# An accumulating transfer in place of a product for the global attention row of a transformer block

## The reference

```python
h = layernorm(x) * (1 + ca) + sa            # ca, sa, ga: one row of 512 per sequence
xs = h.reshape(4, 16, 128, 512)             # segments of 128 tokens
local = softmax(Q K^T * SCALE) V            # inside each segment
summ = xs[:, :, 0, :]                       # the first token of each segment
global_out = softmax(Qg Kg^T * SCALE) Vg    # among the 16 first tokens of a sequence
out = local + global_out[:, :, None, :]     # one row is added to all 128 tokens of a segment
x = x + ga * (out @ Wo.T + bo)              # ga: gate row, at least 0.25 in size
```

## Time and profile before

| | |
|---|---|
| median of 3 runs | 1911.46 us (1911.04 to 1913.74) |
| the profiled execution, its own time | 1909.39 us |
| span of that execution, first to last instruction | 1907.7 us |
| TensorE busy | 1821.5 us, 95% |
| DVE busy | 1226.4 us, 64% |
| POOL busy | 869.4 us, 46% |
| ACT busy | 822.3 us, 43% |
| mean granted TensorE clock | 0.985 of full speed |
| HBM read and written | 237.71 MB, 50.72 MB |

### The profile page before, as it was taken

The page is one execution under the profiler, slowest core; times in us unless marked ns, Lnnn a source line. Parts: engine busy times, 40 slices in busy tenths (PEclk is TensorE's granted clock), DMA queues, the critical chain, the costliest instruction groups (busy, mean ns, idle before and its releaser), DMA issues.

```text
span 1907.7 us, 28124 instructions
## 1 busy us (share of the span) xinstructions
PE 1821.5 (95%) x9137; PEld 1490.8 (78%) x9138; DVE 1226.4 (64%) x1877; ACT 822.3 (43%) x1321; POOL 869.4 (46%) x709
## 2 busy tenths in 40 slices
PE   8999999999999729999999999999998999999998
PEld 3477777778778527889888888888887988888886
DVE  4277888888888745455664544547748887454762
ACT  2445455455455314324443333435545654334541
POOL 2035665666666441244442334335636757233632
PEclk9999999999999969999999999999999999999999
DMA  8034234224224423444534354344545555434622
GB/s 271 29 135 156 89 113 153 89 95 170 88 90 149 162 92 108 144 144 166 178 125 154 127 173 139 122 148 163 185 161 180 191 186 187 170 124 154 214 86 66
DMA packets 137915, 270.77 MB, mean 142 GB/s; under 512 B 17633, under 2 KB 18221, under 8 KB 137862
## 3 DMA queue, kind: packets, MB, share of 16 engines
q1 hardware_dynamic: 115338, 221.27, 33.4%
q0 software_dynamic: 22528, 48.86, 8.0%
HBM read 237.71 MB, written 50.72 MB: 151 GB/s over the span
## 4 chain that ended last, share of the span: by engine, by line
PE 80%; DVE 11%; issue 4%; ACT 2%; POOL 1%; DMA 1%; DVEq 0%; POOLq 0%; ACTq 0%; SPq 0%
PE bank L322 23%; PE bank L324 23%; PE bank L323 23%; PE bank L771 2%; PE bank L707 2%; DVE h L1374 1%; DVE prob L1268 1%; DVE stats L1150 1%; DVE xr L1378 1%; PE bank L814 1%; PE bank L564 1%; PE bank L603 1%; DVE ht_lo L1214 1%; PE bank L532 1%; DVE u_lo L1396 1%
## 5 line engine op out<-in xcount | busy, mean ns | idle before, releaser
L1435 DVE TENSOR_TENSOR h_lo<-h_f,h_hi 128x512 fp32r<-128x512 f32 x256 | 223.5, 894 | 362.7 <-ACT h_f L1087 362.4
L1086 ACT ACTIVATE h_hi<-bank,b_col 128x512 fp32r<-128x512 f32 x256 | 176.7, 690 | 597.6 <-PE bank L324 581.8
L322 PE MATMUL bank<-bt_hi,w_hi 128*128 128x512 f32 (+4 forms) x1024 | 360.5, 352 | 8.4 <-DVE w_lo L1406 6.6
L324 PE MATMUL bank<-bt_hi,w_lo 128*128 128x512 f32 (+4 forms) x1024 | 359.5, 351 | 0.0
L323 PE MATMUL bank<-bt_lo,w_hi 128*128 128x512 f32 (+4 forms) x1024 | 359.3, 351 | 0.0
L322 PE MATMUL bank<-w_hi,h_hi 128*128 128x512 f32 x832 | 326.5, 392 | 2.8 <-DVE h_lo L1435 2.4
L323 PE MATMUL bank<-w_lo,h_hi 128*128 128x512 f32 x832 | 324.9, 390 | 0.0
L324 PE MATMUL bank<-w_hi,h_lo 128*128 128x512 f32 x832 | 324.7, 390 | 0.0
L322 PEld LDWEIGHTS bank<-bt_hi,w_hi 128*128 128x128 f32 x1024 | 194.7, 190 | 34.0 <-issue 9.0
L323 PEld LDWEIGHTS bank<-bt_lo,w_hi 128*128 128x128 f32 x1024 | 194.7, 190 | 20.9
L324 PEld LDWEIGHTS bank<-bt_hi,w_lo 128*128 128x128 f32 x1024 | 194.6, 190 | 20.3
(11 more groups left out here) (252 smaller groups left out, 3264.1 us busy)
## 6 DMA issues: line engine op xcount, KB each, us to landing
raw<-in_L_ffn_W_dram SPq DMA_DIRECT2D x128, 1024.0 KB, 6.9
xa<-in_L_attn_x_dram SPq DMA_DIRECT2D x16, 1024.0 KB, 5.4
xr<-in_L_attn_x_dram SPq DMA_DIRECT2D x16, 1024.0 KB, 7.9
out_dram<-xr SPq DMA_DIRECT2D x16, 1024.0 KB, 9.8
h_rows<-h SPq DMA_DIRECT2D x16, 1024.0 KB, 4.3
b_bc<-in_L_ffn_b_dram SPq DMA_DIRECT2D x16, 256.0 KB, 6.3
wm_b<-in_L_wmod_dram SPq DMA_DIRECT2D x2, 1024.0 KB, 8.2
wm_d<-in_L_wmod_dram SPq DMA_DIRECT2D x2, 1024.0 KB, 5.2
```

The source lines that it names most:

```text
L322: pe.matmul(o, a_hi, b_hi, start=start, stop=False)
L324: return pe.matmul(o, a_lo, b_hi, start=False, stop=stop)
L1086: act.activation(h1_hi[b % 2][:, j, :], h_bank[j][:, :], ACT.Relu, bias=bias)
L1435: dve.tensor_tensor(h1_lo[b % 2][:, j, :], h1_f[:, j, :], h1_hi[b % 2][:, j, :].bitcast(F32), ALU.subtract) \
```

## The change

The gated global row is added to the residual instead of the bank. The prologue loads the floored gate row of each sequence back from HBM to the 16 partitions of its segments (`g_ga`), DVE multiplies the global rows by it in float32, and SP stores the 64 rows (`global_rows`, now float32, one row each). In the attention phase POOL, at the head of its iteration, waits for the load of `xr` of group i-1 and issues one transfer that reads the group's four rows for every partition and adds them to `xr` (1 MB, `accum_op=ALU.add`). DVE waits for that transfer (`xr_summed`) ahead of the first gate product in place of the load. Gone are line 735's product, `seg_sel`, `grows`, its loads and the three parts.

```diff
-    global_dram = nc.dram_tensor("global_rows", (NSEG * 3, D), BF16, kind="Internal").ap()
+    global_dram = nc.dram_tensor("global_rows", (NSEG, D), F32, kind="Internal").ap()
...
-    seg_sel = keep("seg_sel", [P, GS, P], BF16)
-    grows = [keep(f"grows{i}", [P, D], BF16) for i in range(2)]
...
@@ sync
-        sp.wait_ge(g_split_done, 1)
-        sp.dma_start(global_dram.rearrange("(n t) d -> n t d", t=3), g_split[:]).then_inc(g_stored, 16)
-
         sp.wait_ge(mod_fixed, 2)
         sp.dma_start(mod_dram[:, 0:VC, :], modr[:, 0:VC, :]).then_inc(mod_stored, 16)
         sp.wait_ge(mod_stored, 16)
+        for b in range(NBATCH):
+            seg = slice(b * (NSEG // NBATCH), (b + 1) * (NSEG // NBATCH))
+            sp.dma_start(g_ga[seg, :], mod_dram[b:b + 1, GA, :].to_broadcast([NSEG // NBATCH, D])).then_inc(g_ga_in, 16)
 
         sp.wait_ge(pro_evac, PRO_END)
         sp.dma_start(ga_tab[:], spread(GA, P)).then_inc(late_tab_in, 16)
+        sp.wait_ge(g_gated, 1)
+        sp.dma_start(global_dram, g_ga[:]).then_inc(g_stored, 16)
         sp.wait_ge(g_stored, 16)
         sp.dma_start(cb_tab[:], spread(CB, P)).then_inc(late_tab_in, 16)
...
             if cur:
-                wait_past(sp, av_full, 4 * i.n - 4)
-                sp.dma_start(grows[i.par][0:3 * GS, :], global_dram[bass.ds(i.n * 3 * GS, 3 * GS), :]) \
-                    .then_inc(grows_in[i.par], 16)
@@ tensor
-                pe.wait_ge(grows_in[p1.par], 16 * (p1.half + 1))
...
-                    split3(pe, big[s][:, :], pt_hi[:, s, :], pt_lo[:, s, :], u_hi[:, s, :], u_lo[:, s, :], True, False)
-                    pe.matmul(big[s][:, :], seg_sel[:, s, :], grows[p1.par][:], start=False, stop=True) \
+                    split3(pe, big[s][:, :], pt_hi[:, s, :], pt_lo[:, s, :], u_hi[:, s, :], u_lo[:, s, :], True, True) \
                         .then_inc(av_full, 1)
@@ vector
-        dve.memset(grows[0][:], 0.0).then_inc(init_made, 1)
-        dve.memset(grows[1][:], 0.0).then_inc(init_made, 1)
...
-        dve.wait_ge(pro_evac, TG + 1)
-        dve.tensor_copy(g_split[:, 0, :], g_a[:]).then_inc(gsum_step, 1)
-        dve.wait_ge(gsum_step, 8)
-        dve.tensor_tensor(g_x[:], g_a[:], g_split[:, 0, :], ALU.subtract).then_inc(gsum_step, 1)
-        dve.wait_ge(gsum_step, 9)
-        dve.tensor_copy(g_split[:, 1, :], g_x[:]).then_inc(gsum_step, 1)
-        dve.wait_ge(gsum_step, 10)
-        dve.tensor_tensor(g_split[:, 2, :], g_x[:], g_split[:, 1, :], ALU.subtract).then_inc(g_split_done, 1)
         floor_gate(GB)
         dve.sem_inc(mod_fixed, 1)
         dve.wait_ge(pro_evac, PRO_END)
+        dve.wait_ge(g_ga_in, 16 * NBATCH)
+        dve.tensor_tensor(g_ga[:], g_a[:], g_ga[:], ALU.mult).then_inc(g_gated, 1)
         dve.wait_ge(tab_in, 16)
...
-                dve.wait_ge(xr_in[p1.par], 16 * (p1.half + 1))
+                dve.wait_ge(xr_summed[p1.par], 16 * (p1.half + 1))
@@ gpsimd
-        pool.memset(seg_sel[:], 1.0).then_inc(made, 1)
...
         def iteration(i, prev, nxt, prev3):
             p1 = i.plus(-1)
             b = batch_of(p1)
+            if prev:
+
+                if isinstance(i.n, int) and i.n == 1:
+                    pool.wait_ge(g_stored, 16)
+                pool.wait_ge(xr_in[p1.par], 16 * (p1.half + 1))
+                stand_alone(pool, pool_passed)
+                part = global_dram[bass.ds(p1.n * GS, GS), :].unsqueeze(0).to_broadcast([P, GS, D])
+                pool.dma_start(xr[p1.par][:], part, accum_op=ALU.add).then_inc(xr_summed[p1.par], 16)
             if nxt:
                 normalise1(i.plus(1))
```

More of the change, by code:

```diff
@@ L198, in build_block @@
                                       ("bqk", [NBATCH, 2, D], F32), ("hg_t", [P, KC, NSEG], F32))
-    g_split, brow, u_row, gg_t = over(r_tab + 8 * KB, ("g_split", [NSEG, 3, D], BF16), ("brow", [1, D], F32),
+    g_ga, brow, u_row, gg_t = over(r_tab + 8 * KB, ("g_ga", [NSEG, D], F32), ("brow", [1, D], F32),
                                       ("u_row", [1, D], F32), ("gg_t", [P, KC, NSEG], F32))
@@ L261, in build_block @@
     gsum_masked, gsum_negb, gsum_exp, gsum_prob = (sem(f"gsum_{k}") for k in ("masked", "negb", "exp", "prob"))
-    g_split_done, g_stored, table_cleared = sem("g_split_done"), sem("g_stored"), sem("table_cleared")
+    g_ga_in, g_gated, g_stored, table_cleared = (sem(k) for k in ("g_ga_in", "g_gated", "g_stored", "table_cleared"))
     x_in = [sem(f"x_in{i}") for i in range(2)]
     xr_in = [sem(f"xr_in{i}") for i in range(2)]
-    grows_in = [sem(f"grows_in{i}") for i in range(2)]
+    xr_summed = [sem(f"xr_summed{i}") for i in range(2)]
     ln1_step, ln1_ready, ln1_rstd, xn_done = (sem(k) for k in ("ln1_step", "ln1_ready", "ln1_rstd", "xn_done"))
@@ L335, in build_block @@
     LAST_POOL_SEG = GS - 1
-    POOL_MADE = 9
-    DVE_MADE = 8
+    POOL_MADE = 6
+    DVE_MADE = 6
     def results_done(eng, e, b):
@@ L1273, in query_const @@
                 .then_inc(qc_ready, 1)
-        dve.wait_ge(g_split_done, 1)
         tok4 = [P, GS, E]
@@ L1532, in _ @@
         pool.memset(ones[:], 1.0).then_inc(made, 1)
-        pool.memset(seg_sel[:], 1.0).then_inc(made, 1)
-        pool.wait_ge(made, 3)
+        pool.wait_ge(made, 2)
         pool.affine_select(out=tri[:], in_=tri[:], compare_op=ALU.is_gt, fill=0.0, base=0, pattern=[[1, P]],
                            channel_multiplier=-1).then_inc(made, 1)
[L1539 to L1543, removed]
         pool.iota(tokids[:], pattern=[[P, NSEG]], base=0, channel_multiplier=1).then_inc(made, 1)
```

## The result

The changed kernel took 1920.44 us (median of 6 runs, 1918.90 to 1922.78), the kernel before 1912.91 beside it (6 runs, 1911.04 to 1913.74): a ratio of 1.0041, interval 1.0028 to 1.0054. It is slower by 7.5 us. The prediction had 1928 with a range of 1912 to 1975, slower with a chance of 0.83. The direction was right and the measured time lies in the range; the forecast change, 16.3 us, was twice the measured 7.5. The profiled execution took 1919.15 us, its span 1917.5 against 1907.7, its mean granted clock 0.981 against 0.985.

What follows compares the result with a forecast made beforehand. DVE's chain up to u_lo was taken to pace the groups, though TensorE is busiest. Terms -1, +6.6, +1.7, +1, +6 and +2 sum to +16.3 us on 1911.46: 1928 us, range 1912 to 1975.

Steps and rivals of the forecast that it cites:

- The prologue, +6.6 and +1.7: Before the first group: DVE's wait for gate rows and product delay statistics 6.6 us; TensorE's half clock afterwards adds 1.7.
- hidden: Prologue: first xr load goes near 114, the sum lands by 133, before DVE wants it at 133.9.
- The transfer's price, 10.8 us from POOL's end to landing: Steady groups: issuing 1.3, h2 store 2.7, moving 5.4, landing 1.4; sum there 0.6 us ahead of DVE.
- Forecast (A): Whole kernel: transfer hidden but for the last group, 1928 us, own range 1916 to 1938; chance 0.47.
- (B): Attention phase: the sum comes late in every group, 1957 us, at the high ends 1983; chance 0.36.
- The slots of L735, -1: Attention loop: DVE's five waits for L735 give back one slot each, 1.2 us at most, taken as 1.
- rival (C): Attention loop: TensorE is the bound, u_lo is there before it reaches L603; all 64 slots return, 1905 us; chance 0.07.
- The sign that was asked for: Attention loop: distance of L1374 from group to group unchanged near 36 us, 499 in 14 groups.
- The second group, +1: Second group of the attention phase: margin of 9.9 us where the transfer needs 10.8, so 1 us late.
- Collisions of POOL and DVE, +2: Four early groups: POOL's L1608 comes sooner and lengthens the fourth query constant, 0 to 4.4 us, taken as 2.
- The last group, +6: End of attention phase: weight loads take half the DMA engines, moving doubles to 10.8 us, sum 6 us late.
- Its sign of being wrong: Last group: the prediction is wrong if the weight loads leave the transfer its full rate.

Runs made afterwards that it cites:

- Experiment 7: Prologue of experiment 6 and last transfer of experiment 8, with cb and sb tables loaded behind the store of the gated global row: 1908.29 us, 0.9985 to the kernel before.
- experiment 5: Changed kernel with DVE's product of global row and gate moved behind group 0's statistics, u_lo and query constants: 1919.5 us, ratio 1.0041 to the kernel before.
- experiment 3: Changed kernel with the transfer copying the rows over xr instead of adding them; only the attention phase compared: 14 distances 499.47 us against 500.00.
- experiment 4: Changed kernel with POOL issuing the transfer behind the four normalisations of its iteration instead of ahead of them: 2037.97 us in one run.
- experiment 1: Changed kernel with a fourth product per segment, of ones with zeros, put back on TensorE: 1923.72 us, ratio 1.0064 to the kernel before.
- experiment 2: Changed kernel without the accumulating transfer, DVE waiting for the xr load; only the attention phase compared: 1910.42 us, ratio 0.9992 to the kernel before.
- experiment 9: Changed kernel with the first expert weights' loads held back until the last group's transfer has landed: 1920.48 us in one run.
- experiment 6: Changed kernel with experiment 5's later product, its operand in own memory, first xr load behind the tables, product's store behind group 2's x load: 1916.11 us, ratio 1.0020.
- experiment 8: Changed kernel with the last group's accumulating transfer alone issued one iteration earlier: 1918.45 us, ratio 1.0028 to the kernel before.

## Why the prediction was right, and where it was too large

- **The prologue, +6.6 and +1.7: right in the mechanism, a little small.** The statistics were late by 7.73, of which 1.25 was there ahead of the change's first transfer, so 6.5. The half clock cost 1.5, but 2.6 in three kernels with the same prologue, more than the upper bound of 2. Together 8.9 to 9.2 for 8.3. Experiment 7 takes all of it away by order alone. What the prediction missed is that the same delay lay twice, in DVE's order and in SP's queue: it wrote of the first xr load "hidden" with 0.9 us to spare, and experiment 5 shows it as the next wait, once the first is gone.
- **The transfer's price, 10.8 us from POOL's end to landing: right within 0.7.** Measured 10.1. Its parts: issuing 1.0 for 1.3, moving 5.1 for 5.4. The Trainium skill ("Collectives: The Full Stack", the bandwidth ceiling and the fold count) gives the ratio of 1.93, with two source reads as its reason, for collectives over a ring of cores; carried over to this transfer it makes 5.2 as an estimate. The trace's 5.1 is near that, but against the same rows as a plain copy (experiment 3) the measured ratio is 1.74, and that decides here. Whether the second read or the adding costs the time, no run here separates. The slack was 1.4 us in the steady group shown, forecast as 0.6. Forecast (A) holds, and (B) was near: experiment 4, with the issue later, lost 7.9 us a group.
- **The slots of L735, -1: too small.** The loop gained 2.8 us. Most of 15.4 became TensorE's wait for u_lo, as predicted (7.4 to 20.3 us; with a product back it is 9.3), but the term took only the five waits of DVE for L735, and experiment 1 prices the products at 3.6 us. The missing part lies where TensorE waited little or not at all for u_lo: rival (C)'s condition held in three of the 14 distances. The transfer takes some 1.1 of it back (experiment 2). The sign that was asked for, 499 us from group 2 to 16 unchanged, came (499.11 before, 498.73 after), but only because the loop's gain and the last group's loss meet in it.
- **The second group, +1: right.** DVE waited for the transfer, which landed after 10.9 us where 10.8 were forecast. The distance went from 34.63 to 35.13; without the transfer it is 34.30, so it costs 0.8.
- **Collisions of POOL and DVE, +2: none seen.** The fourth query constant did come to 1.65 us in all 15 groups, from 0.69 in the four early ones, but the four distances that hold these became shorter by 0.7 together (groups 2 to 3 fell from 36.65 to 35.39). TensorE waited for u_lo in all four afterwards, 1.1 to 1.8 us, so the longer instruction may have eaten a part of what the slots gave there; no run separates the two.
- **The last group, +6: measured 2.9, the step that failed.** The prediction gave the transfer half of the engines beside the weight loads and so doubled its 5.4. In the trace the transfer kept nearly all of them once it ran beside the loads (85.6% against 17.4% from 662 to 668 us), and it landed only 0.9 us later than with the loads held back (experiment 9). Its sign of being wrong, that the weight loads leave the transfer its full rate, came nearly true. The group was late all the same, because of a term that the prediction counts in every other group and left out here, the 2.7 us of the h2 store ahead of the transfer: the full price of 10.8 less the margin of 7.6 is 3.2 late without any weight load, where the prediction has 0.5 for a transfer that is served first. Experiment 9 has 2.0 (a distance of 32.90 against 30.92). So the lateness is mostly the transfer's ordinary price against a thin margin, and the weight loads, which were to bring the 6, added 0.9.

Terms as measured in the profiled executions: +9.2 in the prologue (6.5 late statistics, 1.5 half clock, 1.2 scatter of the start), -2.8 in the loop with second group and collisions in it, +2.9 at the end, +0.45 behind: 9.8, where 16.3 was predicted. Of the 6.5 between them the last group has 3.1 and the loop 4.8 (+2 predicted, -2.8 measured); the prologue and the end take 1.4 back. The other 2.3 down to the 7.5 between medians are the scatter of the two executions, so the sum's error is no better known than by some 2 us.

Not settled: in eleven of the 14 distances the four products of a group still cost 0.15 us by experiment 1, though TensorE waits for u_lo there; no wait explains it. Nor was a version tried in which DVE's chain is shorter, so whether the rest of the 15.4 us can be had stays open. And why the clock of one run of experiment 7 was low stays open too.

## What to carry to other kernels

Work taken from the busiest engine comes back only where its part of the chain sets the pace; find the wait behind it first, and expect that wait to grow. When a value moves from an engine to a transfer, price the whole chain of its operands as well (load, product, store, load, sum), and read each in-order queue that it passes: a wait in SP's queue held back all loads behind it (experiment 5), and a small store landed the later, the more bytes were issued ahead of it (experiments 5 to 7). The edit was worth keeping only with its transfers in another order: 0.9985 to the kernel before instead of 1.0041, a gain of 2.8 us.

## What the runs showed of the hardware

- An accumulating transfer of 1 MB (one run of 8 KB for each of 128 partitions) kept the 16 engines busy for 5.1 us, the same as a copy for 2.9. It landed 10.1 us after issue beside a 1 MB store, and after 8.0 and 7.7 in experiments 6 and 8, where nothing ran beside it. Issuing took POOL 1.0 us, for the copy 0.66.
- Two queues did not share evenly. Beside the accumulating transfer the weight loads nearly stood for six us (17.4% of the engines against 85.6%, 225 GB/s in all, 394 behind it), and it lost 0.9 us; the h2 store beside it took 5.1, beside the plain copy 8.0.
- A store of 128 KB took 2.7 us to land when the 1 MB issued 6.3 us ahead of it had landed, 6.5 with 3 MB issued ahead and 11.6 with 5 MB (experiments 5, 7 and 6).
- The half clock behind 8.4 to 8.5 us of TensorE's idle time cost between 1.5 and 2.6 us up to the first gate product, in kernels with the same prologue.
